# Position scores of an attention kernel: the read from DRAM issued three units behind the write in place of one

## What is computed

```
y   = gelu(x @ W' + ...)                        # per batch, low-rank terms folded in
q,k,v = y @ Wq, y @ Wkv                         # 16 heads of 64
dist = clip(i - j, -64, 64) + 64                # i, j over 256 positions
pos_attn[i, j] = q[i] . rel_emb[dist[i, j]]     # for each batch and head
attn = softmax((q k^T + pos_attn) * 64**-0.5)
x1  = x + (attn @ v) @ Wo + bo
h_t = GRU step(h_{t-1}, x1_t)                   # t = 0..255, one after the other
out = x1 + mixture of 8 experts(h)              # one expert a token
```

## Time and profile before

| | us |
|---|---|
| median of 3 runs | 760.3 (759.01 to 761.73) |
| profiled execution, span | 755.7 |
| outside its span, against the median | 4.6 |
| TensorE busy | 640.4 (85%) |
| VectorE busy | 461.1 (61%) |
| ScalarE busy | 324.6 (43%) |
| GpSimd busy | 178.0 (24%) |
| SyncE's DMA queue, share of 16 engines | 16.6% |

### The profile page before, as it was taken

The page is one execution under the profiler, slowest core; times in us unless marked ns, Lnnn a source line. Parts: engine busy times, 40 slices in busy tenths (PEclk is TensorE's granted clock), DMA queues, the critical chain, the costliest instruction groups (busy, mean ns, idle before and its releaser), DMA issues.

```text
span 755.7 us, 26078 instructions
## 1 busy us (share of the span) xinstructions
PE 640.4 (85%) x7909; PEld 528.5 (70%) x7909; DVE 461.1 (61%) x3362; ACT 324.6 (43%) x1253; POOL 178.0 (24%) x789
## 2 busy tenths in 40 slices
PE   5998677656788888988889898889888889999995
PEld 4445566545677877877778787778777667877774
DVE  1536344343267777777777777777767556777663
ACT  2356434434145546455555555464544222322321
POOL 1023222221033232232232332322311001111110
PEclk9999967899589999999999999999999999999997
DMA  8022222222212221222212221212210000000000
GB/s 221 9 85 76 85 88 79 92 79 79 76 40 67 74 69 65 67 71 68 71 64 65 74 64 65 74 64 67 72 62 3 2 2 2 10 6 3 4 6 8
DMA packets 43965, 43.06 MB, mean 57 GB/s; under 512 B 5500, under 2 KB 43656, under 8 KB 43784
## 3 DMA queue, kind: packets, MB, share of 16 engines
q1 hardware_dynamic: 43328, 40.75, 16.6%
q10 hardware_dynamic: 584, 1.64, 0.6%
HBM read 20.95 MB, written 21.43 MB: 56 GB/s over the span
## 4 chain that ended last, share of the span: by engine, by line
PE 54%; DVE 14%; DMA 14%; issue 9%; ACT 7%; SPq 1%; DVEq 1%; ACTq 0%; POOLq 0%; POOL 0%
DMA skew<-e_sb 13%; PE bank L622 12%; PE bank L635 12%; PE bank L423 7%; PE bank L407 6%; DVE s_sb L845 3%; ACT hh L765 3%; PE bank L440 2%; DVE g L996 2%; DVE q L988 2%; ACT oT L651 2%; PE bank L455 2%; PE bank L527 2%; PE bank L457 2%; PE bank L453 2%
## 5 line engine op out<-in xcount | busy, mean ns | idle before, releaser
L355 POOL COPY x_nat<-d 128x4 f32 (+1 forms) x256 | 53.5, 209 | 395.7 <-DVE d L1001 395.7
L635 PE MATMUL bank<-q,uc 128*128 128x54 f32 (+1 forms) x512 | 106.1, 289 | 43.3 <-DVE q L988 40.8
L635 PEld LDWEIGHTS bank<-q,uc 128*128 128x128 f32 x512 | 77.7, 190 | 90.3 <-DVE q L988 85.6
L622 PE MATMUL bank<-g,uw 128*128 128x54 f16 (+1 forms) x2560 | 119.1, 189 | 3.6 <-DVE g L996 3.6
L755 ACT ACTIVATE trz<-bank 128x8 f32<-128x8 f32 x256 | 45.5, 178 | 167.9 <-PE bank L622 167.6
L622 PEld LDWEIGHTS bank<-g,uw 128*128 128x128 bf16 x2560 | 103.6, 97 | 17.1 <-DVE g L996 7.9
L622 PE MATMUL bank<-b,uw 128*128 128x54 f16 (+1 forms) x2560 | 110.1, 188 | 0.0
L651 ACT ACTIVATE e_sb<-bank 128x132 f32<-128x132 f32 (+1 forms) x256 | 84.2, 382 | 57.6 <-DMA skew<-e_sb 55.5
L622 PEld LDWEIGHTS bank<-b,uw 128*128 128x128 bf16 x2560 | 108.1, 103 | 1.0 <-issue 0.2
L765 ACT ACTIVATE hh<-bank 128x4 f32<-128x4 f32 x256 | 44.5, 174 | 135.7 <-PE bank L635 131.3
L996 DVE TENSOR_TENSOR g<-z,hh 128x4 f16<-128x4 f32 x256 | 41.9, 164 | 97.5 <-ACT hh L765 97.5
(11 more groups left out here) (133 smaller groups left out, 1054.4 us busy)
## 6 DMA issues: line engine op xcount, KB each, us to landing
skew<-e_sb SPq DMA_DIRECT2D x128, 159.5 KB, 2.7
pos<-skew SPq DMA_DIRECT2D x128, 128.0 KB
wkv_sb<-in_L_attn_Wkv ACTq DMA_DIRECT2D x1, 1024.0 KB, 8.3
x_nat<-in_x SPq DMA_DIRECT2D x1, 512.0 KB, 4.6
wq_sb<-in_L_attn_Wq ACTq DMA_DIRECT2D x1, 512.0 KB, 5.3
wo_sb<-in_L_attn_Wo SPq DMA_DIRECT2D x1, 512.0 KB, 7.3
out<-y_out SPq DMA_DIRECT2D x8, 64.0 KB
ffn_nat<-in_L_ffn_w_gate SPq DMA_DIRECT2D x1, 256.0 KB
```

The source lines that it names most:

```text
L622: ins = mm(out_, uw[:, gate, use, j, :], operand, start=False, stop=True, skip_group_check=True)
L635: mm(c_cols(k, n), uc[:, :], st["q8"][:, now, 0:n], start=False, stop=True, skip_group_check=True).then_inc(c_pre, 1)
```

## The change

The read of a unit is issued three units behind its store (`BEHIND = 3`), and this runs on over the group's edge: beside the stores of units 0, 1 and 2 of a group stand the reads of units 5, 6 and 7 of the group before. The last three reads stand behind the loop. The waits in `skew_unit` and `unskew_unit` are as before.

```diff
@@ -43,6 +43,7 @@
 PERIOD = 16
 BLOCK = PERIOD // 2
 EARLY = 5
+BEHIND = 3
 OVERLAP = GROUPS - EARLY
@@ -275,16 +276,19 @@
-            def skew_group(g):
-                for u in range(PAIRS + 1):
-                    if u < PAIRS:
-                        skew_unit(g, u)
-                    if u:
-                        unskew_unit(g, u - 1)
-
-            skew_group(0)
+            for u in range(PAIRS):
+                skew_unit(0, u)
+                if u >= BEHIND:
+                    unskew_unit(0, u - BEHIND)
             with sp.Fori(0, GROUPS - 1) as i:
-                skew_group(i + 1)
+                for u in range(PAIRS):
+                    skew_unit(i + 1, u)
+                    if u >= BEHIND:
+                        unskew_unit(i + 1, u - BEHIND)
+                    else:
+                        unskew_unit(i, PAIRS - BEHIND + u)
+            for u in range(PAIRS - BEHIND, PAIRS):
+                unskew_unit(GROUPS - 1, u)
```

## The result

The changed kernel takes 753.88 us in the median of 8 runs (751.77 to 756.36), against 759.65 us (758.12 to 762.62, 8 runs) for the kernel before: a ratio of **0.9921, 95% interval 0.9897 to 0.9944**, 5.8 us less. The prediction was 754.3 us, 6.0 less. It was taken from one execution of 755.7 us of span; the profiled execution after has 749.6.

The account below looks back on a forecast made before the run. The prediction took the pair of DMA engines serving reads, idle 2.56 us at each group's edge, to bound the attention stage. -10.2 + 1.5 + 2.8 = -5.9, or -6.0, from 760.3 gave 754.3 us, range 748.5 to 757.5.

Parts of the forecast that it names:

- What bounds the stage: Attention stage before the recurrence: about two of 16 DMA engines serve the reads and pace it, 3.21 us a unit.
- Steady stretch: Four group edges between store (1,2) and store (5,2): the queue no longer drains, 2.56 us saved each, -10.2 us.
- SyncE on a full queue is no loss: SyncE's issues in the steady stretch: they may block with more transfers queued, 1.03 us in place of 0.33, costing nothing.
- backlog of 9.6 us: DMA queue when store n - 3 lands: three reads and three stores stand behind it, about 9.6 us of work.
- R: Service time of one 128 KB read on its pair of DMA engines: 2.87 us, against 0.34 for a store.
- Start: Reads (0,5) to (0,7) now go behind group 1's first stores, so store (1,2) lands later: +1.5 us.
- Late reads: End of the attention stage: the last score, unit (4,7), waits for its read, delaying exp (4,7): +2.8 us.
- The tail: From exp (4,7) to the recurrence: same chain, moves as a block; zero taken for the clock.
- rival 1: More regained, 751 us (748.5 to 752): clock holds in the tail or the score's read wait is absorbed; chance 0.18.
- The recurrence: Stage from 205 us: 4.2 us a unit, above 3.21, so reads two units later cost zero.
- Rival 2: Group edge not closed while start and late reads are paid: 764.5 us, slower; chance 0.07.
- Rival 3: Reads are latency, not engine time, and overlap freely: about 725 us; chance 0.03.

Follow-up runs that it names:

- three with a drain: Kernel before with reads three units behind their stores, but each group's last three reads issued at its end, before the next group's first store: 756.49 us, ratio 0.9967.

## Why the prediction was right

The total was right: 6.0 us forecast, 5.8 measured, and the time of 754.3 lies 0.4 us from the median. That it is so close is in part luck: the interval of the ratio leaves 4.3 to 7.8 us, and of the profiled pair 4.8 us belong to the change. By the forecast's steps:

**What bounds the stage**: shown. The beat of 3.21 us stayed with one, two, three and five reads behind, and went when the read was split. That the queue was service, not latency, is the point on which the sum turned.

**Steady stretch, -10.2 us**: right in mechanism and size. Groups of 25.65 to 25.68 us were measured, 25.68 forecast. But it was put down to three reads in the queue; one read over the edge is enough, and three with a drain close only 3.5 us of it.

**SyncE on a full queue is no loss**: right, but it is the rule and not the exception: nearly every store's issue takes 2.3 to 2.6 us. The backlog of 9.6 us is therefore not reached. When store (1,2) lands at 76.45, two reads are in the queue and not three; the later one, (1,0), has its score start at 82.55, some 6 us on. Nor is the time to landing all service: read (1,0) of the kernel before, issued at 69.25 with no other read in the queue, lands 5.6 us later, of which R = 2.87 us keep the pair from the next.

**Start, +1.5 us**: right in kind, a size that was off: 2.5 us. Store (1,2) lands 12.16 us after exp (0,0), 9.68 before. The forecast took 6.08 us from a read on an idle pair to the landing of the store behind it; here it was 6.99, from 66.25 (read (0,5)) to 73.24 (store (1,1)), as the first read itself is late (6.63 for 5.7). Why it is stays open. What the forecast also didn't see is how much a better start could give: 6.0 us with group 0's reads early, half of it with one behind.

**Late reads, +2.8 us**: right in mechanism and size. The read lands 2.80 us after the store against R = 2.87, and exp (4,7) starts 3.39 us after store (5,2) in place of 0.63, so 2.76 us. With two behind it is 0.62 again, and five behind pays 6.4 us more than three, two beats of 3.21.

The stage is thus -10.3 + 2.5 + 2.8 = -5.0 us, where -10.2 + 1.5 + 2.8 = -5.9 was forecast.

**The tail**: forecast as moving in a block. It grew by 0.55 us: the last transpose waits 2.36 us for `o_sb`, because VectorE's normalisation now stands behind the late score (1.00 us from exp to transpose, 0.70 before), and the clock granted there is 0.51 in place of 0.56, which leaves 0.25 us that no run separates. With one or two behind the clock there is 0.81 and the tail 9.3 us, so rival 1's gain by the clock is real, but of 1.1 us and in other kernels than this one.

**The recurrence, zero**: right, 556.10 against 556.38. Five behind shows where that ends.

Rival 2 (the edge not closed, slower) is out by the groups of 25.7 us. Rival 3, which took the read for latency, is out for this read as it stands: the beat stayed at 3.21 us with one to five reads behind. The price in the Trainium skill (DMA: Bandwidth & Descriptors, "Anatomy of one DMA"), 2.0 us and bytes over 436 GB/s, is given there for DMAs that GpSimd issues, while SyncE issues these. It doesn't hold for this read: by it an estimate would be 2.3 us, and with no read ahead it took 5.6. The size of rival 3 was that of removing the pair's load: the split kernels reach it.

## What to carry to other kernels

When a queue's beat is service, count the transfers that stand before the last one that matters, and see whether the queue ever runs dry: moving a transfer out of an idle stretch into the full one costs its whole service time. At a loop's edge, issue the last dependent transfer behind the first independent one of the next round; depth beyond what keeps the queue fed only delays its users, here by about a beat for each unit beyond two. And look at the rate of a single transfer first: a flat 47 GB/s at a tenth of the engines' time, where the neighbours reach 300, asks for another pattern, and that was worth 45 us where the reordering was worth 6.

## What the runs showed of the hardware

SyncE's queue blocks the issue when two or three reads of this pattern are issued and have not landed (two at 68.25 us in the kernel after, three at 77.52): the issue of a store then takes 2.3 to 2.6 us instead of 0.33. Two are not always enough: in the middle of a group the kernel with one behind issues a store behind two such reads in 0.40 us. In the steady stretch of the kernel after it ends some 0.7 us after the score of a read that has landed starts (82.55 and 83.26, 85.71 and 86.38 us). Such a stop shows in no list of waits, only in the time of the issue. How it is counted, by DMAs or by rows, was not tried.

The outermost dimension of 2 in the pattern of a 128-partition read kept it at 47 GB/s; as two DMAs of 64 plain rows the same bytes no longer bounded anything. That it is the leading dimension of 2 which does it, and not another trait of that pattern, is inferred from this one pair of kernels, the rate and the two late semaphore updates of a read; the Trainium skill (DMA: Bandwidth & Descriptors, "Why a DMA increments its semaphore by 16 and not by 1") states the rule: the number of engines is the largest up to 16 that divides the slowest dimension of both sides. By it 2 and 128 give 2 engines, 64 and 64 give 16, and the trace agrees (a flat 47 GB/s for a read before, and two updates at its landing against sixteen for each half).
